# Moving three quarters of ff2's lower weight half from VectorE to GpSimd, with the orders of head and tail written anew

## The reference

```
y = layernorm(x)
y = layernorm(y + attention(y, y, y, causal), g1, beta1)
y = layernorm(y + attention(y, ctx, ctx), g2, beta2)
y = layernorm(y + relu(y @ w1 + b1) @ w2 + b2, g3, beta3)
x = x + y
xq, wq = fp4(layernorm(x)), fp4(w_gate, w_up, w_down)
x = x + fp4(silu(xq @ wq_gate) * (xq @ wq_up)) @ wq_down
```

## Time and profile before

| what | value |
|---|---|
| median of 3 runs | 596.07 us (595.23 to 597.59) |
| the profiled execution | 594.27 us |
| its span, first to last instruction | 592.4 us |
| mean granted TensorE clock | 0.994 of full speed |
| DMA over the span | 19.31 MB, mean 33 GB/s |

### The profile page before, as it was taken

The page is one execution under the profiler, slowest core; times in us unless marked ns, Lnnn a source line. Parts: engine busy times, 40 slices in busy tenths (PEclk is TensorE's granted clock), DMA queues, the critical chain, the costliest instruction groups (busy, mean ns, idle before and its releaser), DMA issues.

```text
span 592.4 us, 12500 instructions
## 1 busy us (share of the span) xinstructions
PE 555.3 (94%) x4042; PEld 529.0 (89%) x4042; DVE 477.2 (81%) x1222; ACT 372.0 (63%) x778; POOL 387.8 (65%) x463
## 2 busy tenths in 40 slices
PE   4687899999999999999999999999999999899885
PEld 2576799999999999999999999999999999889885
DVE  4989888787878878797878878797878878787776
ACT  3766575867667665867667665867667764746331
POOL 3658776675867766675867766675867666666532
PEclk9998999999999999999999999999999999999989
DMA  7701010010101010010101010010201010000000
GB/s 225 249 2 37 0 46 1 3 53 1 63 3 55 2 44 19 2 51 0 62 0 53 0 44 18 5 48 0 62 2 37 2 36 1 19 2 19 0 11 28
DMA packets 18743, 19.31 MB, mean 33 GB/s; under 512 B 1536, under 2 KB 18192, under 8 KB 18704
## 3 DMA queue, kind: packets, MB, share of 16 engines
q1 hardware_dynamic: 18704, 18.82, 10.3%
HBM read 14.62 MB, written 4.19 MB: 32 GB/s over the span
## 4 chain that ended last, share of the span: by engine, by line
PE 59%; DVE 14%; issue 6%; ACT 5%; POOL 5%; DVEq 0%; ACTq 0%; POOLq 0%
PE O L1180 5%; PE TR L1032 4%; PE R L1198 4%; PE R L1200 4%; PE R L1199 4%; PE R L1032 4%; PE O L1226 3%; PE O L1228 3%; PE O L1227 3%; PE R L1127 3%; PE R L1129 3%; PE R L1128 3%; PE O L1251 3%; PE O L1252 2%; PE O L1253 2%
## 5 line engine op out<-in xcount | busy, mean ns | idle before, releaser
L466 POOL TENSOR_TENSOR rs<-mv,neg_half 128x1 f32<-128x1 f32 (+1 forms) x112 | 70.4, 630 | 32.3 <-DVE mv L1604 32.3
L1198 PE MATMUL R<-y2T_hi,w_hi 128*128 128x256 f32 x256 | 77.1, 301 | 3.4 <-DVE y2T_lo L1732 1.7
L1127 PE MATMUL R<-gu_hi,xqT_hi 128*128 128x352 f32 x240 | 78.9, 329 | 0.4 <-DVE xqT_lo L1678 0.4
L1129 PE MATMUL R<-gu_hi,xqT_lo 128*128 128x352 f32 x240 | 77.3, 322 | 0.0
L1128 PE MATMUL R<-gu_lo,xqT_hi 128*128 128x352 f32 x240 | 77.2, 322 | 0.0
L1251 PE MATMUL O<-w_hi,hT_hi 128*128 128x256 f32 x256 | 73.7, 288 | 1.1 <-POOL hT_lo L501 1.1
L1200 PE MATMUL R<-y2T_hi,w_lo 128*128 128x256 f32 x256 | 72.6, 284 | 0.0
L1199 PE MATMUL R<-y2T_lo,w_hi 128*128 128x256 f32 x256 | 72.6, 284 | 0.0
L1253 PE MATMUL O<-w_hi,hT_lo 128*128 128x256 f32 x256 | 71.8, 280 | 0.0
L1252 PE MATMUL O<-w_lo,hT_hi 128*128 128x256 f32 x256 | 71.7, 280 | 0.0
L591 POOL TENSOR_TENSOR xq<-xa,x_div 128x256 f32<-128x256 f32 x32 | 26.4, 824 | 63.4 <-DVE xa L1673 63.4
(11 more groups left out here) (194 smaller groups left out, 1858.6 us busy)
## 6 DMA issues: line engine op xcount, KB each, us to landing
x_in<-in_x SPq DMA_DIRECT2D x16, 256.0 KB, 2.8
x_res<-in_x SPq DMA_DIRECT2D x16, 256.0 KB, 2.8
out<-x SPq DMA_DIRECT2D x32, 128.0 KB, 1.9
ctx_rows<-in_ctx SPq DMA_DIRECT2D x16, 64.0 KB, 2.5
hT<-in_L_xattn_w SPq DMA_DIRECT2D x1, 1024.0 KB, 8.7
hh<-in_L_xattn_w SPq DMA_DIRECT2D x1, 768.0 KB, 7.6
wd_raw<-in_L_ffn_w_down SPq DMA_DIRECT2D x1, 704.0 KB, 8.9
w_raw<-in_L_ffn_w_gate SPq DMA_DIRECT2D x1, 640.0 KB, 4.6
```

The costliest lines, as they stand in the source:

```text
L466: pool.tensor_tensor(rs[i][:, t0:t0 + len(ts)], mv[i][:, t0:t0 + len(ts), 1], neg_half[:, 0:len(ts)], ALU.pow).then_inc(ln_rstd[i], 1)
L1127: mm(o, xh, gu_hi[:, c, m, cols], start=(c == 0), stop=False)
L1129: last = mm(o, xl, gu_hi[:, c, m, cols], start=False, stop=(c == KC - 1))
L1198: mm(o, w1_hi[:, c, cols], y2T_hi[:, c, :], start=(c == 0), stop=False)
```

## The change

GpSimd gets a function `w2_lower`, the same subtraction as VectorE's, and runs it for the first piece of ff2's weight (1536 columns) between `w_unscaled(1)` and `power(2, 0, 1)`; VectorE keeps the second piece. The lists `head` and `tail` of the four engines that compute are put in another order. Instructions otherwise stay the same, no transfer is added, and `slot` isn't touched. `@@` gives the line before; lines that stay the same stand as context where another was put in or taken out behind them.

```diff
@@ -610 @@
  scale_x(b, g, 0)
+ unscale_x(b, g, 0)
  power(3, b, g, F, (1,))
- unscale_x(b, g, 0)
...
  unscale_x(b, g, 1)
+ scale_h(b, h, 0)
  unscale_h(b, g, 1)
- scale_h(b, h, 0)
@@ -625 @@
+ def w2_lower(i):
+ raw, f0, f1 = w2_raw[i]
+ pool.wait_ge(w2_hi_set, i + 1)
+ pool.tensor_tensor(w2_lo[:, f0:f1, :], raw, w2_hi[:, f0:f1, :].bitcast(F32),
+ ALU.subtract).then_inc(w2_lo_set, 1)
...
  w_scaled(0)
+ power(0, 0, 1, 0, (0, 1))
  masks(0, 0)
- power(0, 0, 1, 0, (0, 1))
- after_shift(0, 0, 1, 0)
+ w_unscaled(0)
  w_scaled(1)
- w_unscaled(0)
  power(1, 0, 1, A, (0, 1))
- after_shift(1, 0, 1, A)
+ masks(0, 1)
+ shift2_row_set()
...
  y_rows(0, 1, True, 0)
+ after_shift(1, 0, 1, A)
  y_rows(0, 1, True, 1)
- masks(0, 1)
  w_unscaled(1)
+ w2_lower(0)
  power(2, 0, 1, A, (0, 1))
- after_shift(2, 0, 1, A)
- shift2_row_set()
...
  power(0, 0, 2, 0, (0, 1))
- after_shift(1, 1, 0, A)
- after_shift(0, 0, 2, 0)
+ context_values(1)
...
  w_scaled(3)
+ after_shift(1, 1, 0, A)
+ pool.wait_ge(rows3_in, 16 * 2)
+ residual(1, 0)
  w_unscaled(2)
+ w_unscaled(3)
+ after_shift(2, 0, 1, A)
...
  y_rows(1, 0, True, 1)
- w_unscaled(3)
  masks(1, 0)
- pool.wait_ge(rows3_in, 16 * 2)
- residual(1, 0)
- context_values(1)
+ after_shift(0, 0, 1, 0)
  h_lower_last(1, 0)
+ after_shift(0, 0, 2, 0)
  power(2, 1, 0, A, (0, 1))
- after_shift(2, 1, 0, A)
...
  power(3, 1, 0, F, (0,))
+ after_shift(2, 1, 0, A)
@@ -946 @@
  last_norm(b, g, 0)
- abs_rows(b, g, 1)
...
  xT_upper(b, h, 0)
+ abs_rows(b, g, 1)
+ last_silu(b, h, 0, 0)
  last_norm(b, g, 1)
- last_silu(b, h, 0, 0)
+ last_silu(b, h, 0, 1)
  abs_x(b, g, 1)
- last_silu(b, h, 0, 1)
...
  part_lifted_abs(b, h, 0)
+ last_upper(b, h)
  part_lifted_abs(b, h, 1)
- last_upper(b, h)
...
  copy_y0T(0, 0)
+ w_abs(0)
  exp_scores(0, 0)
- w_abs(0)
...
  norm_x(0, 1)
- w_abs(1)
...
  w1_upper(0)
+ exp_scores(0, 1)
+ w_abs(1)
  norm(1, 0, 1, A, 0, 1, z1[:, 0, :], z1[:, 0, :])
+ w1_upper(1)
  norm(1, 0, 1, A, 1, 1, z1[:, 1, :], z1[:, 1, :])
- exp_scores(0, 1)
  affine_turned(0, 1, A, n1_turned, y1T, g1_col, beta1_col, y1T_set)
+ exp_cross(0, 1)
+ context_upper(0)
  w_upper(act, 0)
- w1_upper(1)
- context_upper(0)
- exp_cross(0, 1)
  cp_upper(0, 1)
+ w2_upper(0)
  exp_rest(0, 1)
- w2_upper(0)
...
  y2T_upper(1, 0)
+ norm(1, 1, 0, A, 0, 1, z1[:, 0, :], z1[:, 0, :])
  w_upper(act, 1)
- norm(1, 1, 0, A, 0, 1, z1[:, 0, :], z1[:, 0, :])
- norm(1, 1, 0, A, 1, 1, z1[:, 1, :], z1[:, 1, :])
...
  relu(1, 0, (0,))
+ norm(1, 1, 0, A, 1, 1, z1[:, 1, :], z1[:, 1, :])
  copy_y0T(1, 0)
+ relu_upper(1, 0, (0,))
  w_abs(2)
- relu_upper(1, 0, (0,))
+ w_abs(3)
...
  shift2_upper()
- w_abs(3)
- relu(1, 0, (1,))
...
  w2_upper(1)
+ relu(1, 0, (1, 2))
...
  exp_cross(1, 0)
- relu(1, 0, (2,))
...
  w_upper(act, 2)
+ w_abs(4)
  norm(2, 1, 0, A, 0, 1, z2[:, 0, :], z2[:, 0, :])
+ context_turned(1)
+ w_upper(act, 3)
+ context_upper(1)
  norm(2, 1, 0, A, 1, 1, z2[:, 1, :], z2[:, 1, :])
- context_turned(1)
- context_upper(1)
- w_upper(act, 3)
- w_abs(4)
@@ -1445 @@
  last_gate_up(b, h, 1, 1)
+ last_turn(b, h)
...
  down_run(b, g, 1, 0, FIRST_RUN)
- last_turn(b, h)
@@ -1460 @@
  scores(0, 0)
+ values(0, 1, 0)
  turn_context(0)
- values(0, 1, 0)
  values(0, 1, 1)
+ fold_b1(0)
...
  scores(0, 1)
- fold_b1(0)
+ scores_rest(0, 1, (0,))
+ fold_b1(1)
+ scores_rest(0, 1, (1,))
+ w_turn(0, 0, 0, 0)
  turn_z1(0, 1)
- w_turn(0, 0, 0, 0)
  cross(0, 1)
- scores_rest(0, 1, (0,))
  turn_cross(0, 1)
- scores_rest(0, 1, (1,))
- fold_b1(1)
+ fold_b1(2)
  cross_values(0, 1)
+ w_turn(1, 0, 2, 1)
+ values(1, 0, 0)
+ values(1, 0, 1)
+ fold_b1(3)
+ turn_z2(1, 0)
+ ready_for_ff1(1, 0)
+ ff1(1, 0, (0,))
...
  keep_busy(TR[1][:], 4)
- values(1, 0, 0)
- values(1, 0, 1)
- turn_z2(1, 0)
- w_turn(1, 0, 2, 1)
- fold_b1(2)
- fold_b1(3)
- ready_for_ff1(1, 0)
- ff1(1, 0, (0, 1))
+ ff1(1, 0, (1,))
@@ -1491 @@
  scores(1, 0)
+ ff1(1, 0, (4,))
  cross(1, 0)
- ff1(1, 0, (4, 5))
+ pe.wait_ge(b1_fold_set, 1)
+ turn_context(1)
+ ff1(1, 0, (5, 6))
+ w_turn(2, FC // 2, 0, 0)
  turn_cross(1, 0)
- ff1(1, 0, (6, 7))
+ ff1(1, 0, (7,))
  cross_values(1, 0)
- w_turn(2, FC // 2, 0, 0)
...
  ff2(1, 0, 0, range(FF2_CUT))
+ w_turn(3, FC, HEAD, 0)
  ff2(1, 0, 0, range(FF2_CUT, FC))
- pe.wait_ge(b1_fold_set, 1)
- turn_context(1)
- w_turn(3, FC, HEAD, 0)
@@ -1985 @@
  z3_stats(b, g, 0)
+ h_scale(b, g, 1)
...
  aggregate(4, b, g, F, 0)
- h_scale(b, g, 1)
+ ff_sum(b, g, 1)
...
  last_shift(b, g, 0)
- ff_sum(b, g, 1)
@@ -2003 @@
  scaled_sum(b, g, 1)
+ xT_lower(b, h, 0)
...
  aggregate(4, b, g, F, 1)
- xT_lower(b, h, 0)
...
  x_max(b, g, 1)
+ last_product(b, h, 0, 0)
  x_scale(b, g, 1)
+ rows_drop(b, g, 1)
  x_reciprocal(b, g, 1)
- last_product(b, h, 0, 0)
+ last_product(b, h, 0, 1)
  last_max(b, h, 0, 0)
+ last_max(b, h, 0, 1)
...
  x_drop(b, g, 1)
- rows_drop(b, g, 1)
- last_product(b, h, 0, 1)
+ last_scale(b, h)
  xT_lower(b, h, 1)
- last_max(b, h, 0, 1)
- last_scale(b, h)
- down_add(b, g, 0)
...
  last_max(b, h, 1, 0)
+ rows_lift(b, h, 0)
  part_scale(0)
+ rows_drop(b, h, 0)
  split_lower(b, g)
- rows_lift(b, h, 0)
- rows_drop(b, h, 0)
...
  last_max(b, h, 1, 1)
+ down_add(b, g, 0)
+ part_lift(0)
  part_scale(1)
- part_lift(0)
...
  last_lower(b, h)
+ part_lift(1)
  down_add(b, g, 1)
- part_lift(1)
...
  part_lower(0)
+ part_lower(1)
  down_add(b, h, 0)
- part_lower(1)
@@ -2080 @@
  shift(1, 0, 1, A, (0, 1))
+ w1_lower(0)
  w_lift(1)
- w1_lower(0)
+ x_stats(0, 2)
+ w1_lower(1)
+ cross_max(0, 1)
+ w_amax(2)
+ cross_reciprocal(0, 1)
  w_drop(1)
+ cp_lower(0, 1)
+ ctx_lower(0)
  w_lower(0)
- cross_max(0, 1)
- w1_lower(1)
- ctx_lower(0)
- cp_lower(0, 1)
- cross_reciprocal(0, 1)
- w_amax(2)
+ aggregate(0, 0, 2, 0, 0)
+ w_amax(3)
...
  cross_stats(0, 1)
- x_stats(0, 2)
+ aggregate(0, 0, 2, 0, 1)
+ self_part(1, 0, 0)
  shift(2, 0, 1, A, (0, 1))
- self_part(1, 0, 0)
- w_amax(3)
...
  self_stats(1, 0)
- aggregate(0, 0, 2, 0, 0)
- aggregate(0, 0, 2, 0, 1)
...
  shift(1, 1, 0, A, (0, 1))
+ w_reciprocal(1)
  shift(0, 0, 2, 0, (0, 1))
- w_reciprocal(1)
+ w_lower(1)
  b1_folded()
- w2_lower(0)
- w_lower(1)
+ h_lower(1, 0, (0,))
...
  w_drop(2)
- h_lower(1, 0, (0,))
- cross_max(1, 0)
...
  w_lift(3)
+ cross_max(1, 0)
  w_drop(3)
+ w2_lower(1)
+ w_amax(4)
  h_lower(1, 0, (1,))
+ cross_reciprocal(1, 0)
  cp_lower(1, 0)
- cross_reciprocal(1, 0)
- w2_lower(1)
...
  cross_stats(1, 0)
- w_amax(4)
  w_amax(5)
- shift(2, 1, 0, A, (0, 1))
  w_reciprocal(2)
+ x_stats(1, 1)
...
  ff_sum(1, 0, 0)
- x_stats(1, 1)
  z3_stats(1, 0, 0)
+ aggregate(0, 1, 1, 0, 0)
+ shift(2, 1, 0, A, (0, 1))
  aggregate(3, 1, 0, F, 0)
- aggregate(0, 1, 1, 0, 0)
+ w_lift(4)
  aggregate(0, 1, 1, 0, 1)
+ w_drop(4)
  shift(3, 1, 0, F, (0,))
- w_lift(4)
- w_drop(4)
```

## The result

The changed kernel takes 606.37 us (median of 4 runs, 605.21 to 607.29), the kernel before, beside it, 596.83 (595.23 to 598.50): ratio 1.0169, 95% interval 1.0143 to 1.0195. It is 9.5 us slower; forecast were 597.0 us and, with a chance of 0.79, no change. The profiled execution took 605.21 us (594.27 before), its span 602.2 (592.4).

What follows compares the result with a forecast made beforehand. TensorE's matmuls were taken to bound the settled slots, so only head and tail could move: +0.2 head and +0.7 tail make +0.9, added to the median 596.07 give 597.0 us, range 594.2 to 599.6.

Steps and rivals of the forecast that it cites:

- the first of the orders in the head: Head, ScalarE: exp_scores(0,0) follows w_abs(0) and comes at 13.4 in place of 11.80, 1.6 later, delaying masks and first values.
- the row at 14.60: Head, old profile: only 0.66 of 3.45 us busy with the clock at 1.00, taken as a gap without a fall.
- The subtract: Head, GpSimd: 1536 columns in 3.43 us from 30.5, ending at 34.1 before power(2,0,1) at 34.6, so costing nothing.
- Rival 4: Head: GpSimd's subtract takes 5.1 us, power(2,0,1) comes 1.2 later, 598.2 at most; chance 0.06.
- The orders of the head: Head: 3.1 us freed and 3.1 lost through new orders, so a remainder of +0.2 reaches slot 3.
- The lock between VectorE and GpSimd: Shared port pair held exclusively for a whole instruction when VectorE reads two SBUF inputs; head +0.2, by mere sharing -0.5.
- Rival 1: Head, near 46 us: the matmul clock falls and cross(1,0) lies in the slow stretch; +1.0, 598.0; chance 0.16.
- Rival 2: Tail, gate and up: the matmul clock falls; cost 1.6 (598.6) or, over all 24 matmuls, 3.0 (600.0); chance 0.20.
- +0.7 left at the last addition: Tail: new orders delay the second gate and up by 1.8, mostly absorbed; +0.7 remains, bounds 0 and +1.8.
- Rival 3: Head: idle time swallows the early delays, slot 3 starts the whole 3.1 earlier; 593.7; chance 0.12.
- The chances: Whole kernel: no fall 0.46, head fall 0.16, tail fall 0.20, long subtract 0.06, full gain 0.12; no change 0.79.

Runs made afterwards that it cites:

- exp_ctx_first: Changed kernel with exp_scores(0,0) again ahead of w_abs(0) on ScalarE and turn_context(0) ahead of values(0,1,0) on TensorE; ratio 1.0114 to the kernel before.
- head_tail_filled: Changed kernel, all orders untouched, with dummy matmuls (2, 2 and 3 round the cross attention) in the waits of head and tail; ratio 1.0035 to the kernel before.
- old_lean: Kernel before with three dummy matmuls behind cross(1,0) and keep_busy 22 in place of 17 in the tail; ratio 0.9992, median 595.35 us.
- before_filled: Kernel before with the subtract moved, w2_upper(0) ahead of exp_rest(0,1), and dummy matmuls (four, seven, seven, keep_busy 23); ratio 0.9998 to the kernel before.
- both_filled: gap_filled plus 4, 5 and 7 dummy matmuls in TensorE's three waits round the cross attention; ratio 1.0112 to the kernel before.
- gap_filled: Changed kernel, orders untouched, with six dummy matmuls behind scores(0,0), in the wait ahead of the first values; ratio 1.0081 to the kernel before.
- tail_filled: Changed kernel with dummy matmuls in the tail's waits alone (keep_busy 23 in place of 17, then 4 and 6); ratio 1.0095 to the kernel before.

## Why the prediction was wrong

The step that failed is the first of the orders in the head: "`exp_scores(0,0)` ... 13.4, 1.6 later" was priced as a shift of 1.6 and handed down, and nothing was asked about what TensorE does in the meantime. It came at 13.45, to the letter; but with `turn_context(0)` put behind the values the longer wait left TensorE idle for 3 us, and matmuls at half speed for the next 10. At slot 3 the head was forecast +0.2 later; it was 6.3, of which filling this one gap gives back 4.1 (72.75 less 68.67). I had looked for the clock in two places, 46 us and the tail, with the row at 14.60 as evidence that a gap at that place does no harm. But in that execution of the kernel before the clock had risen by 13 us, and the stretch just ahead of the row held 2.03 of 3.10 busy:

```profile
13.03 1.57 PE L1180 MATMUL O<-y,e_diag 128*128 128x257 f32 x6 [0.86 <-POOL e_diag L496]
```

```profile
11.70:14.80 3.10, 2.03 (x9) 1.00 1.07 381
```

In exp_ctx_first the same six take 2.94, at half speed. The change empties just that stretch (0.06 busy).

With the clock held up, the other steps can be compared one by one. Starts in us; the last column is head_tail_filled, whose orders are those of the change:

| instruction | before | forecast | changed | waits filled |
|---|---|---|---|---|
| `exp_scores(0,0)` | 11.80 | 13.4 | 13.45 | 13.49 |
| GpSimd's subtract | none | 30.5 | 34.75 | 30.68 |
| `cross_sum(0,1)` | 29.45 | 32.5 | 36.77 | 32.70 |
| `power(2,0,1)` | 31.53 | 34.6 | 38.84 | 34.77 |
| ff1, first matmul | 36.60 | 39.4 | 44.81 | 39.78 |
| `exp_scores(1,0)` | 45.74 | 47.25 | 52.95 | 47.92 |
| `cross_values(1,0)` | 51.09 | 54.25 | 60.20 | 55.16 |
| `y2T_lower`, slot 3 | 66.41 | 66.7 | 72.75 | 67.70 |

- **The subtract**: right, in its length, its place against its neighbours and its cost of nothing. Rival 4 is out. (30.5 and 3.43 make 33.9 and not the 34.1 of the working; it began at 30.68 and ended at 34.18.)
- **The orders of the head**: within 0.4 up to ff1, 1.0 too early at slot 3. Of the 6.3 that the head lost, 5.05 (72.75 less 67.70) is the clock and 1.3 the orders; against old_lean (65.70), where the low clock at 46 is gone as well, the orders cost 2.0.
- **The lock between VectorE and GpSimd**: right. `ctx_lower` waited for GpSimd's product and took 1.14. In the tail `part_scale(0)` (384 columns) started at 588.53 under a VectorE product of 588.28 to 589.11 and took 1.27 (0.84 before).
- **Rival 1** (the clock falls at 46): the mechanism was right, the place wrong, and its price 5 in place of 1.
- **Rival 2** (it falls in the tail): it did, under both pieces. The tail lost 2.05. The step "+0.7 left at the last addition" was not seen: with a clock of 1.00 throughout, the new tail takes 31.13 (head_tail_filled) and the old one 31.20 (before_filled), so in these two executions the orders cost nothing there and the low clock all of it.
- **Rival 3** (3.1 freed in full): no. In the old lists, with the clock held up, the move gave 1.3 in one execution each; the medians (595.35 and 594.96) do not tell it from nothing.
- **The chances** failed with the step: I gave low clocks 0.36 together and held them for exclusive, each at one place. A list laid out anew has many new waits, and behind four of them the clock was low in one execution.
- **What was not in the forecast at all**: 1.4 in the settled slots, which belongs to the execution, and 1.1 outside the span (3.0 against 1.9).

Open is what the last 2 us of head_tail_filled are; the 2.0 of the new head's orders, by one profile each, would account for them.

## What to carry to other kernels

When an order is changed, add up TensorE's busy time in each stretch that a new wait opens, above all near the start, where its clock has just risen or not yet: an idle gap of 3 us off the critical path cost 4 us here. Read the clock from the durations of like matmuls, and not from the clock column alone. Dummy matmuls in such waits are a cheap test and a cheap cure, as long as they end before the wait does: with groups longer than the waits before_filled shows no gain, and both_filled none over gap_filled.

## What was not expected of the hardware

- The clock column shows 1.00 while matmuls run at 1.2 GHz, until the clock first rises: 2.08 against 1.03 for four 128x257 matmuls.
- Half speed outlasts the gap that brings it: in the changed kernel TensorE was busy 9.51 of the 10.20 us from 14.80 to 25.00, and the clock rose only behind that.
- The same lists rise at different times: half speed lasted to 26 us in the changed kernel's profile and to 30 in tail_filled's, which moved slot 3 by 3.3.
- The settled slots have two prices for one of the two crossings, 33.94 and 34.32, with the clock at 1.00 in both.
